# The attention product with the exponentials streamed: four heads side by side in the array, outputs transposed, sums spread over partitions

## The reference

```python
n = layernorm(x)                                    # rows of 512
q, k, v = n @ Wq.T + bq, ctx @ Wk.T + bk, ctx @ Wv.T + bv     # 16 heads of 32
sm = einsum('nlhd,nshd->nlhs', q, k) / sqrt(32)     # 154 keys
sm = where(triu(ones(L, S), k=1), -inf, sm)         # causal, so only the first 154 rows are masked
attn = einsum('nlhs,nshd->nlhd', softmax(sm), v)
x = x + attn.reshape(N, L, 512) @ Wo.T + bo
h = bit_linear(layernorm(x), w1)                    # rows quantised to 8 bits, weights ternary
h = silu(depthwise_conv1d(h) + conv_b)              # three taps along the sequence
out = x + bit_linear(h, w2)
```

## Time and profile before

| | |
|---|---|
| median of 3 runs | 1537.06 us (1532.29 to 1551.35) |
| the profiled execution | 1532.68 us, its span 1530.9 us |
| mean granted clock of TensorE | 0.972 of full speed |
| busy share of the span | PE 94%, PEld 58%, DVE 85%, ACT 77%, POOL 68% |
| values' product (L852), all of it | 331 us of PE in 2560 instructions |
| turn of the outputs (L940) | 31.8 us of PE |
| reciprocals (L1709) | 15.7 us of DVE in 64 instructions |

### The profile page before, as it was taken

How to read it: one execution, slowest core, us unless ns; L and a number is a source line. 1 busy time by engine, 2 the same in 40 slices (tenths; PEclk the granted TensorE clock), 3 DMA queues, 4 the chain that set the end, 5 groups by cost and what they waited for, 6 DMA issues and landing times.

```text
span 1530.9 us, 24697 instructions
## 1 busy us (share of the span) xinstructions
PE 1446.2 (94%) x9025; PEld 887.7 (58%) x9025; DVE 1296.1 (85%) x2014; ACT 1184.0 (77%) x2176; POOL 1036.5 (68%) x838
## 2 busy tenths in 40 slices
PE   8998988999999999999999999999999999998866
PEld 5474655657575656656575656656575756565322
DVE  7777796898979898898979898898979898978796
ACT  3567788979687888879687888889687978887752
POOL 4011567868676978968676869878776869777552
PEclk8989899999999999999999999999999999998987
DMA  8551002030311203031201103031302111020000
GB/s 257 151 187 42 29 7 70 8 96 17 74 43 25 80 8 98 8 101 21 75 32 46 59 8 98 8 102 29 81 17 63 43 27 51 8 70 1 31 28 29
DMA packets 80343, 85.20 MB, mean 56 GB/s; under 512 B 29983, under 2 KB 55839, under 8 KB 79709
## 3 DMA queue, kind: packets, MB, share of 16 engines
q1 hardware_dynamic: 80221, 83.62, 18.9%
HBM read 38.74 MB, written 19.42 MB: 38 GB/s over the span
## 4 chain that ended last, share of the span: by engine, by line
PE 70%; DVE 17%; ACT 9%; issue 3%; POOL 1%; DMA 0%; DVEq 0%; ACTq 0%; SPq 0%
PE ps L852 13%; PE ps L679 12%; PE ps L950 11%; DVE negm L1742 11%; PE ps L858 10%; PE ps L1036 9%; ACT hqb L1156 4%; ACT pexp L1235 3%; PE ps L821 3%; DVE h L1658 2%; PE ps L940 2%; PE ps L918 1%; PE ps L1006 1%; PE ps L827 1%; PE ps L1020 1%
## 5 line engine op out<-in xcount | busy, mean ns | idle before, releaser
L644 POOL TENSOR_TENSOR h<-h,gall 128x512 f32<-128x512 f32 x235 | 349.2, 1486 | 18.4
L654 POOL TENSOR_TENSOR h<-h,r 128x512 f32<-128x512 f32 x240 | 307.0, 1332 | 58.5 <-ACT r L1156 58.5
L642 POOL TENSOR_TENSOR gall<-gall,cw 128x512 f32<-128x512 f32 x235 | 257.5, 1096 | 110.3 <-DVE h L1658 110.3
L1658 DVE SCALAR_TENSOR_TENSOR h<-gall,cw,h 128x512 f32<-128x512 f32 x256 | 259.9, 1018 | 48.2 <-ACT h L1254 48.0
L852 PEld LDWEIGHTS ps<-va,pexp 128*128 128x128 f32 x2048 | 261.5, 193 | 29.1 <-issue 11.5
L1583 DVE SCALAR_TENSOR_TENSOR gall<-ps,bias,srow 128x512 f32<-128x512 f32 x256 | 191.1, 747 | 89.2 <-POOL h L644 59.2
L858 PE MATMUL ps<-xqT,w1T 128*128 128x512 f16 x1024 | 258.1, 382 | 6.9 <-DVE gall L1583 6.8
L852 PE MATMUL ps<-va,pexp 128*128 128x33 f32 x2048 | 260.0, 271 | 0.0
L1036 PE MATMUL ps<-w2T,hqb 128*128 128x512 fp8e4 x960 | 241.3, 380 | 0.0
L1254 ACT ACTIVATE h<-gall,cb,cw 128x512 f32<-128x512 f32 x256 | 222.0, 867 | 8.5
L1235 ACT ACTIVATE pexp<-ps 128x512 f32<-128x512 f32 x320 | 179.5, 587 | 55.6 <-PE ps L821 27.3
(11 more groups left out here) (220 smaller groups left out, 2303.3 us busy)
## 6 DMA issues: line engine op xcount, KB each, us to landing
qs<-hl SPq DMA_DIRECT2D x192, 128.0 KB, 2.4
xr<-in_x SPq DMA_DIRECT2D x16, 1024.0 KB, 5.4
out<-xr SPq DMA_DIRECT2D x64, 256.0 KB
h<-in_L_ffn_w SPq DMA_DIRECT2D x8, 1024.0 KB, 5.4
srow<-in_L_xattn_bo SPq DMA_DIRECT2D x15, 256.0 KB, 3.3
kst<-kh_scratch SPq DMA_DIRECT2D x32, 38.5 KB
xr<-in_ctx SPq DMA_DIRECT2D x1, 1024.0 KB
h<-in_L_xattn_Wk SPq DMA_DIRECT2D x1, 1024.0 KB, 8.2
```

Source lines behind the costliest of these rows:

```text
L642: gp.tensor_tensor(right, right, cw[:, c, 2:3].to_broadcast([P, TB]), ALU.mult).then_inc(c2m_ok, 1)
L644: gp.tensor_tensor(hc(c), hc(c), right, ALU.add).then_inc(c2p_ok, 1)
L654: gp.tensor_tensor(hc(c), hc(c), r2[:], ALU.mult).then_inc(u_ok, 1)
L1658: ve.scalar_tensor_tensor(out=hc(c), in0=g[:, c % 4, 1:TB + 1], scalar=cw[:, c, 1:2], in1=hc(c), op0=ALU.mult, op1=ALU.add).then_inc(c1_ok, 1)
```

## The change

The values' product is turned round. The exponentials move through the array, 512 columns at a time, and the values stand still. `pv` now has four pieces for a group:

- piece 0: for each head j, the values (128 keys x 32) in columns 32j to 32j + 31 of the array (`tile_position=(0, j * HD)`), output to partitions 32j and on of a bank `obank`
- piece 1: the same with 32 columns of ones, output to another bank `zbank`, so that each sum stands in all 32 partitions of its head
- pieces 2 and 3: the tail tile through a block-diagonal 128 x 128 of values, and through one of ones, added to both banks

These are 10 f32 products of 512 columns for a group, where there were 20 of 33 or 132. They come after the scores of the next group rather than two tiles behind the exponentials; the last group's four pieces follow `turn_x` in one run. The output has channels on partitions already, so `turn_o` is gone, and `at_high` and `at_low` read `osb` in SBUF.

`attention(k)` now takes a reciprocal of 128 x 512 from PSUM and then multiplies, at c = 6, 9, 12 and 14. Twenty tiles of exponentials are spread over `pexp`, `xn`, `osb` and the query buffer `qs`; for that, some waits are added on ACT (`PT_FREE`, `normalise1`), and SP loads the next `qs` once the last piece is done. The constants and `fetch_v` follow the new shapes (the column of ones in `va` goes, `zt` comes); those lines are left out here.

```diff
@@ -147,18 +147,17 @@
         TURN = [A[0], A[1], A[4], A[5]]
-        OT = [A[5], A[4], F[0], F[1]]
         OB = [A[4], A[5], F[0], F[1]]
...
-        def obank(g, half):
-
-            return A[2 + 2 * (g % 2) + half]
-
-        def opair(g):
-
-            return ps[:, 2 + 2 * (g % 2):4 + 2 * (g % 2), 0:2 * J * HV].rearrange("p u (e x) -> p u e x", x=HV)
+        def obank(g):
+
+            return A[2 + 2 * (g % 2)]
+
+        def zbank(g):
+
+            return A[3 + 2 * (g % 2)]
@@ -247,6 +246,11 @@
         kvrow = srow[0:2].bitcast(F16)[:, 0:2 * D].rearrange("p (a t) -> p a t", a=2)
+        qsf = qsv.bitcast(F32).rearrange("p (n t) -> p n t", t=TB)
+        pt = [pexp[:, 0, :], pexp[:, 1, :], pexp[:, 2, :], xn[:, 0, :], xn[:, 1, :],
+              xn[:, 2, :], xn[:, 3, :], osb[:, 2, :], osb[:, 3, :], pexp[:, 0, :],
+              qsf[:, 0, :], qsf[:, 1, :], qsf[:, 2, :], qsf[:, 3, :], osb[:, 3, :],
+              pexp[:, 2, :], qsf[:, 4, :], qsf[:, 5, :], pexp[:, 0, :], pexp[:, 1, :]]
         khl = hqb[:, CT // 2:CT, :].rearrange("p c t -> p (c t)")
@@ -387,6 +390,9 @@
+        NORMALISE = (6, 9, 12, 14)
+        PT_FREE = {9: 2, 14: 6, 18: 8}
+
         def score_tiles(c):
@@ -508,7 +514,7 @@
                         fetch_kb(batch_of + 1)
-                        sp.wait_ge(pv_ok, at(s, NS, NS))
+                        sp.wait_ge(pv_ok, at(s, NP, NP))
                         if s == BPB - 1:
@@ -526,7 +532,7 @@
                     if do_a:
-                        sp.wait_ge(s_ok, at(s, NS, NS))
+                        sp.wait_ge(pv_ok, at(s, NP, NP))
                     for j in range(J):
@@ -830,26 +836,27 @@
-                def pv(i):
-
-                    gi, j = divmod(i, J + 1)
-                    pr = pexp[:, i % 3, :]
-                    if i == 0 and s >= 1:
+                def pv(n):
+
+                    gi, piece = divmod(n, 4)
+                    if n == 0 and s >= 1:
                         pe.wait_ge(src, at(s, 1, 0))
-                    if i == J + 1 and late_results(s - 1):
+                    if n == 4 and late_results(s - 1):
                         pe.wait_ge(out_ok, at(s, 4, -8))
-                    if j == 0 and gi >= 2:
+                    if piece == 0 and gi >= 2:
                         pe.wait_ge(at_ok, at(s, NG, gi - 1))
-                    if s == 0 and j == 0 and gi == 1:
+                    if s == 0 and n == 4:
                         pe.wait_ge(su_kvh, 2 * NG + 1 + NBATCH)
-                    pe.wait_ge(e_ok, at(s, NS, i + 1))
-                    for t in range(TT):
-                        o = obank(gi, t // 2)[:, (t % 2) * J * HV:(t % 2 + 1) * J * HV]
-                        rhs = vt[:, gi, :]
-                        if j < J:
-                            o = o[:, j * HV:(j + 1) * HV]
-                            rhs = va[:, gi * J + j, :]
-                        r = mm(o, pr[:, t * P:(t + 1) * P], rhs, start=j == 0 and t % 2 == 0, stop=j == J, skip_group_check=True)
+                    bank = (obank, zbank)[piece % 2](gi)
+                    if piece < 2:
+                        pe.wait_ge(e_ok, at(s, NS, (J + 1) * gi + J))
+                        for j in range(J):
+                            r = mm(bank[j * HD:(j + 1) * HD, :], onesf[:, 0:HD] if piece else va[:, gi * J + j, :],
+                                   pt[(J + 1) * gi + j], start=True, stop=True, tile_position=(0, j * HD))
+                    else:
+                        pe.wait_ge(e_ok, at(s, NS, (J + 1) * gi + J + 1))
+                        r = mm(bank, zt[:] if piece == 3 else vt[:, gi, :], pt[(J + 1) * gi + J], start=False, stop=True,
+                               skip_group_check=True)
                     r.then_inc(pv_ok, 1)
@@ -927,24 +934,16 @@
-                def turn_o():
-
-                    pe.wait_ge(at_ok, at(s, NG, NG))
-                    for k in range(NG):
-                        if k == 2 and do_f:
-                            pe.wait_ge(g_ok, at(s, CT, 0))
-                        if k == 2 and s == 0:
-                            pe.wait_ge(w_out, CT)
-                            pe.wait_ge(w_scale, 4)
-                        for t in range(TT):
-                            r = tp(OT[k][:, t * P:(t + 1) * P], osb[:, k, t * P:(t + 1) * P], identf[:])
-                        r.then_inc(ot_ok, 1)
-
                 def project_out(i, k):
...
                         pe.wait_ge(al_ok, at(s, NG, max(k + 1, 2)))
+                    if i == 2 and k == 0 and do_f:
+                        pe.wait_ge(g_ok, at(s, CT, 0))
+                    if i == 2 and k == 0 and s == 0:
+                        pe.wait_ge(w_out, CT)
+                        pe.wait_ge(w_scale, 4)
                     bank = OB[i]
@@ -1047,8 +1046,8 @@
                             score(i)
-                            if i >= 2:
-                                pv(i - 2)
+                            if i > J + 1 and i % (J + 1):
+                                pv(4 * (i // (J + 1) - 1) + i % (J + 1) - 1)
                     if s == 0 and 2 <= c < 10:
@@ -1063,8 +1062,8 @@
                     if do_a and c == LASTU + 2:
-                        pv(NS - 2)
-                        pv(NS - 1)
+                        for n in range(NP - 4, NP):
+                            pv(n)
@@ -1230,9 +1227,12 @@
                     act.wait_ge(s_ok, at(s, NS, i + 1))
-                    if i >= 3:
-                        act.wait_ge(pv_ok, at(s, NS, i - 2))
-                    nc.scalar.activation(pexp[:, i % 3, :], A[i % 2], ACT.Exp, scale=1.0 / QS).then_inc(e_ok, 1)
+                    if i == 7 and s == 0:
+                        for q in v_out:
+                            act.wait_ge(q, 64)
+                    if i in PT_FREE:
+                        act.wait_ge(pv_ok, at(s, NP, PT_FREE[i]))
+                    nc.scalar.activation(pt[i], A[i % 2], ACT.Exp, scale=1.0 / QS).then_inc(e_ok, 1)
@@ -1286,6 +1286,8 @@
                         act.wait_ge(ln1, at(s, 7, 14))
+                    if do_a:
+                        act.wait_ge(pv_ok, at(s, NP, 6 if first else 4))
                     if first:
@@ -1330,8 +1332,10 @@
                 def at_high(k):
-                    act.wait_ge(ot_ok, at(s, NG, k + 1))
-                    copy(ah(k), OT[k]).then_inc(ah_ok, 1)
+                    act.wait_ge(at_ok, at(s, NG, k + 1))
+                    if k == 0:
+                        act.wait_ge(pv_ok, at(s, NP, NP))
+                    copy(ah(k), osb[:, k, :]).then_inc(ah_ok, 1)
@@ -1705,20 +1709,21 @@
                 def attention(k):
-                    dve.wait_ge(pv_ok, at(s, NS, (J + 1) * (k + 1)))
-                    ve.reciprocal(rz[:, k], opair(k)[:, :, :, HD]).then_inc(rz_ok, 1)
+                    dve.wait_ge(pv_ok, at(s, NP, 4 * (k + 1)))
                     if k == 0 and s == 0:
...
                         dve.wait_ge(xqt_ok, at(s, KT, 0))
+                    ve.reciprocal(osb[:, k, :], zbank(k)).then_inc(rz_ok, 1)
                     dve.wait_ge(rz_ok, at(s, NG, k + 1))
-                    ve.tensor_tensor(osb[:, k, :].rearrange("p (u e d) -> p u e d", u=2, d=HD), opair(k)[:, :, :, 0:HD],
-                                     rz[:, k].unsqueeze(3).to_broadcast([P, 2, 2 * J, HD]), ALU.mult).then_inc(at_ok, 1)
+                    ve.tensor_tensor(osb[:, k, :], obank(k), osb[:, k, :], ALU.mult).then_inc(at_ok, 1)
                 def at_low(k):
+                    if k == 0 and do_q:
+                        dve.wait_ge(xt_ok, at(s, KT, 2 * KT))
                     dve.wait_ge(ah_ok, at(s, NG, k + 1))
-                    ve.tensor_tensor(al(k), OT[k], ah(k), ALU.subtract).then_inc(al_ok, 1)
+                    ve.tensor_tensor(al(k), osb[:, k, :], ah(k), ALU.subtract).then_inc(al_ok, 1)
@@ -1835,8 +1840,8 @@
                         w_scales(1)
-                    if do_a and c in (4, 7, 10, 14):
-                        attention((c - 4) // 3)
+                    if do_a and c in NORMALISE:
+                        attention(NORMALISE.index(c))
```

More of the change, by code:

```diff
@@ L55, in build @@
     SA = S0 + HD
-    HV = HD + 1
     PAIR = 2 * S
@@ L59, in build @@
     NS = NG * (J + 1)
+    NP = 4 * NG
     assert D == 512 and S0 < S <= SA and BPB == 4 and CG == 4 and TT == 4
@@ L104, in build @@
         kst = sb("kst", [3 * HD + 1, H, SA], F16)
-        va = sb("va", [P, H, HV], F32)
-        vt = sb("vt", [P, NG, J * HV], F32)
+        va = sb("va", [P, H, HD], F32)
+        vt = sb("vt", [P, NG, P], F32)
+        zt = sb("zt", [P, P], F32)
         xr = sb("xr", [P, 5, TT, D], F32)
@@ L126, in build @@
         r2 = sb("r2", [P, TB], F32)
-        rz = sb("rz", [P, NG, 2, 2 * J], F32)
         st1 = sb("st1", [P, TT, 6], F32)
@@ L308, in build @@
         at_ok = sem("at_ok")
-        ot_ok = sem("ot_ok")
         ah_ok = sem("ah_ok")
@@ L472, in fetch_v @@
             def fetch_v(b):
```

(10 more changed lines are left out.)

## The result

Before, in the runs beside it: 1534.67 us, the median of 4 runs (1531.61 to 1551.35). After: 1803.29 us, the median of 4 runs (1801.14 to 1804.72). The ratio is 1.172, with a 95% interval of 1.165 to 1.179. The forecast of 1709 had the direction and the place; the time lies 13 us above its range. The profiled execution after has a span of 1802.8 us and a mean granted clock of 0.919; before it was 1530.9 and 0.97.

A forecast was written before the change was run, and what follows sets the result against it. PE's chain of waits bounds the first part, with POOL and DVE just behind. A later `at_low` adds 11.3 us in 15 slots and 7 in the first, 177 us on 1532.7: 1709 us, range 1640 to 1790.

The forecast's parts named there:

- rival 1: f32 strips on PE overlap fully, pieces take 0.98 us, DVE alone is late: 8.3 us a slot, 1662 us; chance 0.24.
- Side by side: Pieces 0 and 1 on PE: strips start in program order, so four heads take 2.26 us instead of 0.98.
- The last run: The last group's pieces on PE in one run: 5.7 us.
- `at_low` reading SBUF: DVE's `at_low` reads SBUF instead of PSUM: costs nothing, since both have 512 columns as before.
- The clock: PE's idle time might lower its granted clock; named as a way to be wrong, with no time in the sum.
- The reciprocal: DVE in `attention(k)`: 512 columns take 2.9 us, making `attention(k)` 3.6 us instead of 0.95.
- Rival 4: A steeper reciprocal on DVE: 6.9 ns an element, 3.7 us for 512, 1.6 us a slot more, 1733 us; chance 0.05.
- One f32 product of 512 columns: On PE, bound by its columns: 0.43 us an instruction, 0.87 us a product of two.
- the wait of the third step of `turn_x`: On PE, this step waits for `attention(2)`, now at c = 12, with the last pieces and `mm1(14)` behind.
- The turn of the outputs: 16 transposes on PE's path go, 1.75 us; the second part keeps its length without them.
- The 0.7 of slack: DVE has 0.7 us free before the row maxima, so they start 11.0 to 11.7 us later.

The follow-up runs named there:

- e8: Changed kernel with pieces 0 and 1 reordered: each piece does two heads, for each head the values' product, then the ones'; 1808.92 us, a single run.
- e15: Changed kernel with a copy for the reciprocal, `at_low` reading PSUM and `attention(2)` at c = 11, output wrong; 1529.92 us, ratio 0.995.
- e2: Changed kernel with `at_low` subtracting from a PSUM bank instead of `osb` in SBUF, low half wrong; 1731.7 us, ratio 1.122.
- e9: Changed kernel with unused filling matmuls on PE, 12 before `mm1(12)` and 27 before the waiting half of `turn_x`; 1764.6 us, ratio 1.147.
- e16: Changed kernel with `attention(2)` called at c = 11 instead of 12, nothing else, result right; 1740.15 us, ratio 1.132.
- e3: Changed kernel with the last group's four pieces ahead of the half of `turn_x` that waits for `attention(2)`, output the same; 1747.61 us, ratio 1.132.
- e17: Changed kernel with `attention(2)` at c = 11 and 12 filling matmuls each before `mm1(12)` and the third step of `turn_x`; 1735.41 us, ratio 1.130.
- e5: Changed kernel with the reciprocal cut to 512, 256, 128 and 64 columns for groups 0 to 3, the rest copied; 1699.76 us, a single run.
- e10: Changed kernel with POOL's taps for tiles 12 to 15 and its output-bias additions cut to one column; 1715.27 us, ratio 1.115.
- e4: Changed kernel with unused filling matmuls on PE, 12 before `mm1(12)` and 18 before the waiting half of `turn_x`; 1786.45 us, ratio 1.156.

## Why the prediction came out as it did

Set on the start of the slot's first `dequant` (594.63 before, 694.66 after), the steps of the sum were forecast and measured at (us):

| | forecast | rival 1 | measured |
|---|---|---|---|
| `attention(2)` ends | 42.2 | 41.5 | 42.8 |
| half of `turn_x` ends | 43.1 | 42.4 | 44.8 |
| last pieces end | 48.8 | 46.0 | 50.6 |
| `at_low` ends | 60.4 | 57.6 | 66.7 |

From forecast to measured are 6.4 us at the end, 95 in 15 slots, where the median missed by 94. The largest part of it, 3.9, is `at_low`.

**Side by side (pieces 2.26 us): the step that failed by its mechanism.** Starts aren't in program order across strips; a piece takes 0.99 (e8). The last run was forecast at 5.7 and measured 5.79 by luck, because it ran mostly at half the clock; at the upper level it is 1.85 + 1.91 = 3.76 (e15). A mechanism that was wrong thus covered a cost that was left out. Rival 1's mechanism holds, with its time too low by 141 us, since `at_low`, the clock and the reciprocal were as small in it.

**`at_low` reading SBUF (nothing): failed.** It is 1.59 us a step in place of 0.68, 3.9 us a slot on the path; e2 gives 72 us back. I looked at the width of the instruction and not at what POOL does at that moment. The trace of before could have warned: its taps on DVE, two operands in SBUF, take 1.66 us beside POOL and 0.74 without it, and the sum itself used that price, in the 2.5 us for tile 7's two taps. It was not carried over to `at_low`, whose operands the change moves to SBUF while POOL works.

**The clock (named as a risk, priced at nothing): failed.** PE's wait for `attention(2)` was forecast, and is there: 4.23 us, behind one of 3.08 for `dequant(10)`. What the waits do to the work behind them was left out of the sum: 39 us at least (e9).

**The reciprocal (2.9 us): right mechanism, the term mis-sized.** 3.35, 0.45 more each; 1.8 a slot, 27 us. Rival 4 had 3.7 for it. The Trainium skill ("VectorE: DVE Perf Modes", section "First, the fixed hardware budget") has the divide step repeated 8 times; at its 0.96 GHz that gave an estimate of 8.3 ns an element. Measured are 6.25.

**One f32 product of 512 columns (0.43 an instruction), the wait of the third step of `turn_x`: right.** Strip passes start 0.44 us apart, and `turn_x` waits where it was said to. The turn of the outputs is gone, but the second part did not keep its length: with `at_low` and a reciprocal in it, it grew by 3.6 us. What the turn's 1.75 us are worth no run shows. That the place of `attention(2)` could be had for less was not in the prediction: a tile earlier is worth 63 us (e16).

Over rival 1's 8.9 a slot then lie 3.9 of `at_low`, 1.8 of reciprocals, and 3.3 on the half of `turn_x` and the last pieces (1.97 for 0.9 and 5.79 for 3.6; the clock's part is the 2.9 above): 9.0 together, against the table's 66.7 - 57.6 = 9.1. With the 8.9 that is the slot's growth of 18.0. The 0.7 of slack that the prediction saw before the maxima took up nothing: they start 21.8 us after the end of `at_low`, before 21.9.

Shown by runs are: that the reciprocals, `at_low` and the late place of `attention(2)` with the clock behind it carry all of the loss (without the three the kernel is at 0.995 of before, e15), what each gives back alone, that strips overlap, and that place and clock matter. The single gains of 165, 72 and 63 us add up to more than the 269 lost, so they overlap. What the 5 us by which e15 is faster than before consist of stays open; they lie at the edge of what can be told. And no version that computes everything beats the kernel before: the best are e3, e16 and e17, 13% slower. The order of e3 and the place of e16 were not tried together.

## What to carry to other kernels

A sum spread over 512 columns makes the reciprocal 32 times as wide (16 elements before), and that is paid at 6.25 ns an element on the engine that can least afford it; taking work from PE gave next to nothing here: in e15 PE's busy time is 36 us less than before (1446 to 1410) and the time 5. Before an operand moves from PSUM to SBUF, look which engine works beside it, and whether the trace has an instruction of the same kind in that company. And a step that is called a tile too late costs twice when TensorE waits for it: once the wait, and once the slower clock behind it.

## What the runs showed of the hardware

- f32 column strips run fully side by side, and each goes on by itself: 8 instructions of 512 columns in 0.99 us, with starts out of program order across strips (0.01 us apart where a whole head stands between, e8).
- DVE's RECIPROCAL costs 6.25 ns an element and 147 ns, from 64 to 512 columns (e5).
- A DVE TENSOR_TENSOR with both 128x512 operands in SBUF, f32 and f16, takes 1592 ns beside POOL's work on SBUF and 686 with POOL quiet; with the first in PSUM it takes 676 beside POOL's work (e2, e10). Of DVE's taps before, with two f32 tiles in SBUF, one takes 1.66 us beside POOL and one 0.74 without it.
- A wait of 1.91 us in PE's work was followed by 1.2 GHz in some slots and by 2.4 GHz in others, in one and the same kernel (e4). In the changed kernel the granted clock fell 1.5 us after a wait of 3.08 us had ended, and 0.7 us before the end of the next one.
